# Splitting the weighted sum of a recurrent attention into two column tiles of 64 queries a head

## The reference, cut to what matters

```
logfg = log_sigmoid(f_pre);  Fcum = cumsum(logfg)
Dmat  = Fcum[s] - Fcum[t] + i_pre[t], where t <= s, else -inf
m     = max over t;  Smat = exp(Dmat - m)
C     = (q @ k.T / sqrt(16)) * Smat
n     = max(|sum over t of C|, exp(-m))
h     = (C / n) @ v
```

## Time and profile before

| what | value |
|---|---|
| median of 3 runs | 704.68 us (704.48 to 705.83) |
| span of the profiled execution | 703.9 us; its own device time is not listed apart from the three runs |
| TensorE matmuls (PE) | 684.1 us busy, 97% of the span |
| TensorE weight loads (PEld) | 581.4 us busy, 83% |
| DVE | 516.5 us, 73% |
| ACT | 372.7 us, 53% |
| granted TensorE clock | 0.993 over the span; 1.00 of 2.4 GHz from 46 us on |

### The profile page before, as it was taken

One profiled execution on the slowest core, in us unless ns is written; L12 is line 12 of the kernel. 1 busy time (PEld: TensorE's weight loads), 2 busy tenths in 40 slices (PEclk: granted clock), 3 DMA queues, 4 the chain that ended last, 5 costly groups with the idle time before them and its releaser, 6 DMA issues.

```text
span 703.9 us, 10617 instructions
## 1 busy us (share of the span) xinstructions
PE 684.1 (97%) x4040; PEld 581.4 (83%) x4040; DVE 516.5 (73%) x919; ACT 372.7 (53%) x775; POOL 131.7 (19%) x125
## 2 busy tenths in 40 slices
PE   7999999999999999999999999999999999999997
PEld 7878988878777788887888878887777898889886
DVE  7736567886965757557675576657679998989996
ACT  5886776855735425444253442446566455354541
POOL 7144444510000020000200002000123213203220
PEclk8999999999999999999999999999999999999999
DMA  5087443000100000110001100060000000000000
GB/s 194 5 258 245 127 150 99 0 1 1 62 1 30 1 1 8 54 31 1 1 2 61 31 0 1 7 265 1 1 1 0 1 2 31 1 31 1 1 31 31
DMA packets 24002, 31.17 MB, mean 44 GB/s; under 512 B 1232, under 2 KB 19952, under 8 KB 23184
## 3 DMA queue, kind: packets, MB, share of 16 engines
q1 hardware_dynamic: 23296, 29.18, 12.8%
q10 hardware_dynamic: 656, 1.31, 0.5%
HBM read 28.18 MB, written 2.31 MB: 43 GB/s over the span
## 4 chain that ended last, share of the span: by engine, by line
PE 72%; DVE 18%; ACT 5%; issue 2%; POOL 1%; DMA 1%; DVEq 0%
PE bank L89 21%; PE bank L91 20%; PE bank L90 20%; PE bank L511 4%; DVE l_ring_lo L2533 3%; DVE l_ge L2514 2%; DVE l_h L2529 2%; DVE l_o L2537 1%; PE bank L485 1%; DVE h_raw L1212 1%; DVE l_h L2486 1%; PE bank L500 1%; PE bank L516 1%; DVE h_ring_lo L1217 1%; DVE l_oT_lo L2543 1%
## 5 line engine op out<-in xcount | busy, mean ns | idle before, releaser
L1212 DVE TENSOR_TENSOR h_raw<-h_s,bank 128x512 f32<-128x512 f32 x104 | 71.4, 687 | 107.8 <-ACT h_s L1202 93.5
L1202 ACT ACTIVATE h_s<-bank 128x512 f32<-128x512 f32 x104 | 62.3, 599 | 164.0 <-PE bank L91 162.7
L1217 DVE TENSOR_TENSOR h_ring_lo<-h_raw,h_ring_hi 128x512 fp32r<-128x512 f32 x92 | 68.9, 749 | 0.1
L1206 ACT ACTIVATE h_ring_hi<-h_raw 128x512 fp32r<-128x512 f32 x104 | 64.9, 624 | 2.3 <-DVE h_raw L1212 2.3
L90 PE MATMUL bank<-fused_lo,h_ring_hi 128*128 128x256 f32 x208 | 58.4, 281 | 0.0
L2233 ACT ACTIVATE l_s<-bank 128x512 f32<-128x512 f32 x32 | 19.2, 599 | 64.5 <-PE bank L91 64.5
L89 PE MATMUL bank<-l_xT_hi,l_wgu 128*128 128x512 f32 x128 | 51.3, 401 | 0.1
L89 PE MATMUL bank<-f_yT_hi,mlp_hi 128*128 128x512 f32 x128 | 50.6, 395 | 0.0
L90 PE MATMUL bank<-l_xT_lo,l_wgu 128*128 128x512 f32 x128 | 50.3, 393 | 0.0
L91 PE MATMUL bank<-l_xT_hi,l_lo 128*128 128x512 f32 x128 | 50.2, 393 | 0.0
L91 PE MATMUL bank<-f_yT_hi,fused_lo 128*128 128x512 f32 x128 | 50.0, 390 | 0.0
(11 more groups left out here) (372 smaller groups left out, 2013.4 us busy)
## 6 DMA issues: line engine op xcount, KB each, us to landing
m_W<-m_scratch SPq DMA_DIRECT2D x16, 512.0 KB, 6.7
fused_raw<-in_fused SPq DMA_DIRECT2D x1, 3584.0 KB, 11.9
res<-in_x SPq DMA_DIRECT2D x4, 512.0 KB, 6.2
fused_raw<-in_fused SPq DMA_DIRECT2D x2, 1024.0 KB, 8.7
f_mask<-expert_weights SPq DMA_DIRECT2D x8, 256.0 KB
l_raw<-in_layer SPq DMA_DIRECT2D x1, 2048.0 KB, 8.6
out_x<-res SPq DMA_DIRECT2D x16, 128.0 KB, 1.9
f_xw<-in_turned_x SPq DMA_DIRECT2D x3, 512.0 KB, 5.9
```

Of the source, the lines that this page charges most:

```text
L1202: self.nc.scalar.activation(self.s[u % 2][r, :], gate[r, :], ACT.Silu).then_inc(self.silu.sem, 1)
L1206: self.nc.scalar.activation(self.unit(i, u)[0], self.product(i, u), ACT.Copy).then_inc(self.hi.sem, 1)
L1212: self.nc.vector.tensor_tensor(out=self.product(i, u), in0=self.s[u % 2][r, :], in1=up[r, :], op=ALU.mult).then_inc(self.hidden.sem, 1)
L1217: self.nc.vector.tensor_tensor(out=lo, in0=self.product(i, u), in1=f32(hi), op=ALU.subtract).then_inc(self.lo.sem, 1)
```

## The change

It cuts each head's stationary operand of 128 queries into two of 64 queries. The first half writes partitions 0 to 63 of the bank, the second partitions 64 to 127, with the same moving operand. There are 16 matmuls a chunk in the program where there were 8 (32 passes where there were 16), 128 more in all. Nothing else is moved, and no wait is added or taken away.

```diff
     per_head = lambda ap: ap.rearrange("p (h e) -> p h e", e=V1)
+    halves = [slice(r, r + P // 2) for r in range(0, P, P // 2)]
     chunk = lambda c: slice(c * P, (c + 1) * P)
...
             for h in range(H):
-                last = nc.tensor.matmul(n_bank[:, h * V1:(h + 1) * V1], W[n % RING][:, h, :], v1[b % 2][:, c, h * V1:(h + 1) * V1],
-                                        start=h == 0, stop=c == 0, skip_group_check=True)
+                for some in halves:
+                    last = nc.tensor.matmul(n_bank[some, h * V1:(h + 1) * V1], W[n % RING][:, h, some], v1[b % 2][:, c, h * V1:(h + 1) * V1],
+                                            start=h == 0, stop=c == 0, skip_group_check=True)
```

## The result

| | before | after |
|---|---|---|
| median of 6 runs beside each other | 704.66 us (704.48 to 705.83) | 701.61 us (699.87 to 702.59) |
| ratio of the two | | 0.9949, interval 0.9936 to 0.9961 |
| profiled execution | span 703.9 us | 702.44 us, span 700.6 us |
| second measurement, another chip | 704.75 us (17 runs) | 700.63 us (5 runs), ratio 0.9938 (0.9922 to 0.9953) |

The change makes the kernel faster by 0.5 to 0.6%. The kernel before took 704.1 to 704.9 us in such runs (705.44 and 706.58 once each, median 704.6); the changed kernel took 699.87, 699.99 and 700.06.

A forecast was written before the change was run, and what follows sets the result against it. TensorE bounds the kernel except at both ends of the phase, its block by weight loads; gains of 3.5 (ordinary chunks), 1.3 (chunks 3, 7) and 0.35 (14, 15) make 5.1 us, 704.7 to 699.6 us, range 697 to 702.

The forecast's parts named there:

- Loads of two column tiles overlap: Line 511's block: the two tiles' 64-column loads run side by side, 0.060 us a pair; chance with a switch 0.52.
- The rival of turns: Line 511's block: half loads take turns, with a switch, 2.22 us a block, 711.7 us in all; chance 0.22.
- A switch is paid: Entering and leaving column tiles empties TensorE's array and exposes a first load; block 1.26 us, line 516's first pass 0.19 dearer.
- Chunks 1 to 10: Eight ordinary chunks gain 0.44 us each, 3.5 in all; chunks 3 and 7 gain 0.64 each, 1.3 in all.
- Chunks 3 and 7: Blocks behind a score, where the entry was already paid: 0.64 us less each, 1.3 us together, all kept.
- The tightest wait behind them: Projection behind chunks 3 and 7 reads parts DVE ended at 90.89, starts at 91.76; chunk 7's 0.64 fits in 0.87 us.
- its second half: What reaches the end, 5.1 us; wrong if blocks shorten but PE shows new idle time between 50 and 115 us.
- Chunks 11 to 13: No gain: the blocks' 1.7 us become idle time at line 500's wait for m_part, growing from 0.39 to about 2 us.
- Chunks 14 and 15: DVE is full until f_yT_lo ends at 135.71, first gate product starts at 136.13; some 0.35 of 0.9 us gets through.
- The sum: Whole kernel: 3.5 + 1.3 + 0.35 = 5.1 us gained, from 704.7 to 699.6 us.
- The granted clock should stay at 1.00: TensorE's clock stays at 2.4 GHz, as no new gaps of any length arise before 115 us.
- end effect: The runs' median lies 0.8 us above the profiled execution's span, taken as something at the end the change doesn't touch.

## Why the prediction was right, and where it wasn't

**Loads of two column tiles overlap: right.** A pair costs 0.0585 us (forecast 0.060) where a whole load cost 0.112. The rival of turns (its chance was 0.22) is refuted by the chain's 1.05 us. With the halves one after the other it is nearly true, and that kernel had 1.78 us a block, with 0.11 more in the operation behind it, and 706.4 us, where I had 2.22 and 711.7: the passages were priced too high, and the middle of the block overlaps even so. The rule of the Trainium skill weighed there, from "TensorE: Matmul & The Clock Gate", section "Part 3: Packing small matmuls — row/col tiling", which wants different row groups for an overlap, does not hold for column tiles here.

**A switch is paid: right in kind, a little dear.** What the Trainium skill says in "TensorEngine Tiling (Array Packing)", section "Key Properties", that changing the tiling mode drains TensorE, fits the trace: 0.12 us a passage. Block and state product together fell from 1.71 + 0.53 to 1.05 + 0.64, by 0.55 us instead of 0.44. The new block is thus 1.16 us with the cost of leaving, where 1.26 was forecast. Of the 0.10, 15 pairs at 0.0585 instead of 0.060 make 0.02; the rest is the switch, whose terms (0.085 + 0.058 + 0.03 + 0.085 + 0.107 = 0.365) come to 0.28. Line 518 is 0.11 us dearer and not 0.19.

**Chunk 0.** Forecast nothing, since ACT bounds it; measured 0.13 us.

**Chunks 1 to 10.** Forecast 3.5 + 1.3 = 4.8; measured 4.45. Two errors opposed each other. The eight ordinary steps gave 4.6 rather than 3.5 (0.53 to 0.63 each). **Chunks 3 and 7 gave -0.19 rather than 1.3: this step failed.** "The tightest wait behind them is the projection behind chunks 3 and 7" named m_hT_lo and 0.87 us of room. The wait that came is that of the projection of queries for `add(b-1, 0)` (line 1048), which stands in DVE's order behind weights, four normalisations and a mean square. The kernel before showed no wait there, and I did not ask how much room there was. Its trace had the answer: behind chunk 7 the addition ends at 94.60 us, and the product that needs it starts at 94.73. The room was 0.13 us (0.16 behind chunk 3), so that of the 0.65 us by which the block shrank 0.5 turned into idle time, as the third row shows (before, before, and the second profile after):

```profile
93.92 0.68 DVE L1046 TENSOR_TENSOR xn<-bank,xn 128x512 f32<-128x512 f32 x1
94.73 0.42 PE L89 MATMUL bank<-m_yT_hi,wp_hi 128*128 128x512 f32 x1
90.89 0.50 PE L89 MATMUL bank<-m_yT_hi,wp_hi 128*128 128x512 f32 x1 [0.50 <-DVE xn L1048]
```

By the prediction's own sign, new idle time between 50 and 115 us, its second half was wrong in this part. The reordering in the new kernel (1.15 us in two steps) and in the old one (nothing) shows it as made by the change.

**Chunks 11 to 13: right.** Forecast nothing; measured a loss of 0.09 in sum. The wait for m_part grew from 0.39 to 1.57 us, and a new one of 0.67 us came between chunks 12 and 13, ahead of line 486, for DVE's m_W; together 1.85 us, the 1.7 that the forecast had turning into idle time:

```profile
123.87 0.71 PE L501 MATMUL bank<-m_v,m_ktil 128*128 128x264 f32 x2 [1.57 <-DVE m_part L982]
```

**Chunks 14 and 15.** Forecast 0.35, measured 0.45. The first gate product, which before started 0.42 us behind the end of f_yT_lo without waiting for it, now waits 0.41 us for it: the limit is the one that the forecast had named.

**The sum.** 4.9 measured from chunk 0 on against 5.1; least disturbed runs 700.0 against 704.6, a gain of 4.6, where 699.6 had been forecast. That it came so close is luck in part: ordinary chunks gave 1.1 us more than forecast, and chunks 3 and 7 gave 1.5 less. The medians gained only 3.05 and 4.1 us. That of the first measurement is 701.6, inside the forecast's own range by 0.4; five of those six runs had a mean granted clock under 0.997. "The granted clock should stay at 1.00" was said of the time after 46 us and failed there in the first profile. The base for that had been a single profile; the spread of the runs before (1.35 us in three) was a hint. The "end effect" of 0.8 us was misread as well: in every run for which both are known, the time is 1.7 to 2.0 us above the span. So the profiled execution before, with its 703.9 us and a granted clock of 0.993, took about 705.7 us and was itself a disturbed one. The forecast did not suffer, since it took its gain off the median.

## What to carry to other kernels

Where small products are bound by loading weights, two column tiles side by side halved the cost of a load here (0.112 to 0.0585 us) and four nearly halved it again (0.034). What counts then is a passage of 0.12 us at either end of a row of tiled products, and that the tiles alternate in the queue. Before crediting a gain of the bound engine, list for each of its later products how long ago its inputs were ready, also those with no wait now. The smallest such room decides, here 0.13 us. Reordering the other engine may then be worth something: 1.15 us by chunk 8 by one line of DVE's order, which was worth next to nothing before.

## What the runs showed of the hardware

- Loads of different column tiles ran side by side even where each tile's passes stood together in the queue, over the few loads around the change of tile: seven loads in 0.17 us in the middle of a block otherwise at 0.058 us each.
- Four column tiles took eight instructions, four loads and four matmuls, every 0.034 us.
- An operation of DVE that takes 0.41 us took 1.18 beside one of GpSimd's, and whether the two met differed between executions, with the landing of a DMA.
- The stretch of 1.2 GHz at the start of the phase lasted from 37.5 to 47.7 us in one execution of the changed kernel and ended by 42 us in another, with no instruction changed. It moved the time by 2.4 us, half of the effect under study. In four of the twelve profiles of all kernels the clock stayed at 1.00 from 38 to 46 us.
